# A fused four-layer kernel: FP4 weights decoded in three operations, part of it moved into stage 1, and a softplus polynomial split between VectorE and ScalarE

## The chip, the core and the metric

One NeuronCore of one Trainium2 chip runs the whole kernel in one launch. The metric is device time in microseconds (us). Engines: PE is TensorE (matrix products), DVE VectorE, ACT ScalarE, POOL GpSimd, SP SyncE, which issues most of the DMAs. ScalarE evaluates its functions from loaded tables; the compiler places a table load wherever a function of another set follows.

## The reference, cut to what matters

Four layers, each a cross attention and a feed-forward part with a gated residual. x is (4, 256, 256), that is 1024 tokens of 256 features. The change touches the feed-forward part of layer 0 and the state-space part of layer 3, whose context side is computed early.

```python
# layer 0, feed-forward: W = NVFP4_LUT[4-bit code] * scale of its block of 32
Wg = dequant_nvfp4(gate_W_packed, gate_scales)   # (2048, 256); two codes in each int32
Wu = dequant_nvfp4(up_W_packed, up_scales)
Wd = dequant_nvfp4(down_W_packed, down_scales)   # (256, 2048)
x = x + tanh(g_ffn[0]) * ((gelu(h @ Wg.T) * (h @ Wu.T)) @ Wd.T)      # h = layernorm(x)
# layer 3, attention: a state-space scan over the context
dt = softplus(dt_low @ dt_proj_w.T + dt_proj_b)                      # (4, 256, 256)
state = state * exp(dt * A) + (dt * u) * B_t;  y = (state * C_t).sum() + D * u
```

## The kernel before, in words

The kernel is a row of eight stages, each a block in which every engine has its own instruction list, written by hand; waits on semaphores tie the lists together, and a stage begins when all engines have ended the one before. Each engine keeps to the order of its list.

**Stage 0** is the attention of layer 0. SP loads x, the attention's weights and then, through `load_packed` (L191), the packed codes of gate, up and down (1 MB each) with their scales. The whole FP4 decode stands on VectorE, in six pieces of 128x2048 numbers (`dequant_on_vector`, L199): pieces 0 and 1 are the low and the high code of gate, 2 and 3 of up, 4 and 5 of down. A piece is four instructions: two that shift and mask the low 16 bits of each word into magnitude (L206) and sign (L208), an OR (L210), and one that multiplies the result, read as fp16, by 2^14 and the scale (L218). Piece 0 stands before the softmax's normalisation, piece 1 behind it, pieces 2 to 5 behind the update of x (L323), as the last work of the stage.

**Stage 1** is the feed-forward part of layer 0, with the state-space part of layer 3 laid beside it. The hidden dimension of 2048 is cut into 16 blocks (NHC), the tokens into two halves: 32 units u. For each unit TensorE computes `gate_up(u + 1)` (L511) and then `down(u)` (L524); ScalarE takes gelu of the gate (L445, two units at a time), VectorE multiplies by the up part in `gated(u)` (L645). `down(u)` waits for `gated(u)`, `gate_up(u)` for `gated(u - 2)`. Beside it, for the state-space part: the context's projection (L479), a convolution (L560) and Silu, then the projection of B, C and the step (`project_bc`, L487), whose result VectorE splits into three bf16 parts (`split_rows_1` and `_2`, L574 and L582, in units 0 and 1); ScalarE copies it for a store (L450). `project_steps(k)` (L495) gives the argument of softplus for each half k of the 256 channels: in PSUM at units 2 and 3. Softplus is max(z, 0) + log(1 + exp(-|z|)): ScalarE computes Abs and Exp (`step_exponent`, L422, after units 2 and 4), VectorE the clamp at zero (L595) and log(1 + t) as a polynomial of degree 10, Horner's way (`softplus`, L590), in three parts per k, one part in each of the units 3 to 8. From unit 9 (SCAN0) on, 19 scan groups follow, about one per unit (`scan_group`, L624): TensorE broadcasts a row of B and of C (`row`, L467), ScalarE computes the decays exp(dt * A) (L410), VectorE multiplies, scans (L634), multiplies, and POOL issues a DMA that adds the result to yssm (L690). `add_half` (L616) adds the result of each token half to x.

The loads of stage 1 (L403) are issued by SP when the stage begins. Buffers are cut by hand out of the regions regA, regB and regC.

Of the kernel before, what the change touches and what calls it, by code (L numbers as in the profile page):

```python
# [6 lines left out]

# [5 lines left out]
T = B * S  # L13
NT = T // P
KD = D // P
# [12 lines left out]
I32 = mybir.dt.int32  # L28
F32R = mybir.dt.float32r
# [22 lines left out]
def build(nc, a, out):  # L52
    with ExitStack() as ctx:
# [133 lines left out]
        raw = [regB[:, i * 2048:(i + 1) * 2048].bitcast(I32) for i in range(3)]  # L187
        scl = [regB[:, (3 + i) * 2048:(4 + i) * 2048] for i in range(3)]
# [10 lines left out]
        def dequant_on_vector(dve, v, dq, s_pk, pieces):  # L199

            code, sign = dq
            for n in pieces:
                i, par = divmod(n, 2)
                dve.wait_ge(s_pk[i], 16 * 9)
                lo16 = raw[i].bitcast(U16).rearrange("p (n two) -> p n two", two=2)[:, :, 0]
                v.mark(nc.vector.tensor_scalar(code, lo16, 9 - 4 * par, 0x0E00,  # L206
                                               ALU.logical_shift_left, ALU.bitwise_and))
                v.link(nc.vector.tensor_scalar(sign, lo16, 12 - 4 * par, 0x8000,  # L208
                                               ALU.logical_shift_left, ALU.bitwise_and))
                v.link(nc.vector.tensor_tensor(code, code, sign, ALU.bitwise_or))  # L210
                half = code.bitcast(FP16)
# [11 lines left out]
        def stage0():  # L223
# [6 lines left out]
            dq = [ar.take([4 * HALF], U16), ar.take([4 * HALF], U16)]  # L230
# [4 lines left out]
            s_pk = [sem(f"s0_pk{i}") for i in range(3)]  # L235
            s_aTp, s_aT, s_mix, s_v = sem("s0_aTp"), sem("s0_aT"), sem("s0_mix"), sem("s0_v")
            s_tg = sem("s0_gates")
            with nc.Block("stage0") as block:  # L238
# [59 lines left out]
                def _(dve):  # L298
# [26 lines left out]
                    dequant_on_vector(dve, v, dq, s_pk, range(2, 6))  # L325
# [22 lines left out]
        LDEG = len(L) - 1  # L348

# [3 lines left out]
        def stage1():  # L353
# [13 lines left out]
            zpos = arP.take([KD, T])  # L367
            bcf = arP.take([T])
# [6 lines left out]
            bc32 = arB.take([T])  # L375
# [9 lines left out]
            SP = 3  # L385
            SCAN0 = SP + 3 * KD
# [11 lines left out]
            with nc.Block("stage1") as block:  # L398
# [10 lines left out]
                def _(act):  # L409
# [12 lines left out]
                    def step_exponent(k):  # L422
                        act.wait_ge(s_pre, k + 1)
                        w = (sA, sB)[k]
                        nc.scalar.activation(w, pair, ACT.Abs, bias=cw[:, k, TAPS + 1:TAPS + 2]).then_inc(s_e, 1)
                        act.wait_ge(s_e, k + 1)
                        nc.scalar.activation(dt[:, k, :], w, ACT.Exp, scale=-1.0).then_inc(s_dt, 1)

# [11 lines left out]
                    for u in range(0, NU, 2):  # L440
# [6 lines left out]
                        if u == 0:  # L447
                            nc.scalar.activation(alog, alog, ACT.Exp).then_inc(s_A, 1)
                            act.wait_ge(s_bcs, 1)
# [7 lines left out]
                        if u in (2, 4):  # L457
                            step_exponent(u // 2 - 1)
# [7 lines left out]
                def _(pe):  # L466
# [57 lines left out]
                    def down(u):  # L524
                        c = u % NHC
                        pe.wait_ge(s_itm, u + 1)
                        if u == NHC:
# [10 lines left out]
                    for u in range(NU):  # L538
# [6 lines left out]
                        if u == SP - 1:  # L545
                            project_steps(0)
                        down(u)
# [8 lines left out]
                def _(dve):  # L556
# [33 lines left out]
                    def softplus(k, part):  # L590

                        t, q, w = dt[:, k, :], du[:, k, :], (sA, sB)[k]
                        if part == 0:
# [4 lines left out]
                            v.link(nc.vector.tensor_scalar(q, t, -0.5, None, ALU.add))  # L598
                            v.link(nc.vector.tensor_scalar(w, q, L[LDEG], L[LDEG - 1], ALU.mult, ALU.add))
                            v.link(nc.vector.tensor_tensor(w, w, q, ALU.mult))  # L600
                        for c in {0: (8, ), 1: (7, 6, 5, 4), 2: (3, 2, 1)}[part]:
                            v.link(nc.vector.scalar_tensor_tensor(w, w, L[c], q, ALU.add, ALU.mult))
                        if part == 2:
                            v.link(nc.vector.scalar_tensor_tensor(w, w, L[0], t, ALU.add, ALU.mult))
                            dve.wait_ge(s_max, k + 1)
                            v.link(nc.vector.tensor_tensor(t, w, zpos[:, k, :], ALU.add))
# [46 lines left out]
                    for u in range(NU):  # L653
                        if u == 0:
                            split_rows_1()
                        elif u == 1:
                            split_rows_2()
                        elif u == 2:
# [5 lines left out]
                        elif u < SCAN0:  # L664
# [1541 lines left out]
```

## Time and profile before

| | us |
|---|---|
| median of 3 runs | 976.05 |
| lowest and highest | 972.63, 976.88 |
| the profiled execution | 975.31 |
| its span, first to last instruction | 973.5 |
| VectorE busy | 701.5 (72%) |
| TensorE busy | 638.0 (66%) |
| ScalarE busy | 316.7 (33%) |
| mean granted TensorE clock | 0.798 of full |

Times in the rows are microseconds from the span's start. Stage 0 runs to 64.6, stage 1 from there to about 279. A row of a timeline gives the start, the duration, engine, line, operation, output<-input with their shapes, a count if several were merged, and in brackets how long the engine had been idle before it and what ended that.

### The profile page before, as it was taken

The page shows a single profiled execution, that of the slowest core. Times are in us where ns is not written, and L with a number is a line of the kernel's source. Part 1 is how long each engine was busy: PE and PEld are TensorE (multiplying, and loading weights), DVE is VectorE, ACT ScalarE, POOL GpSimd, SP SyncE. Part 2 cuts the span into 40 slices and gives each one's busy share as a digit, 9 for nine tenths or more (in the row PEclk, how much of TensorE's full clock was granted, in tenths as well). Part 3 has the DMA queues.
Part 4 walks back from the last instruction along what each step waited for, and adds up shares of the span by engine and source line. Part 5 has one row for each costly group of instructions (what it writes and reads, how often), then busy time and mean ns, then how long its engine had stood idle before and what let it go on. Part 6 is the DMA issues. An engine that isn't in the chain of part 4 may idle for free. (4 is left out here: it accounts for less than half of the span.)

```text
span 973.5 us, 9330 instructions
## 1 busy us (share of the span) xinstructions
PE 638.0 (66%) x2790; PEld 400.1 (41%) x2793; DVE 701.5 (72%) x1409; ACT 316.7 (33%) x535; POOL 188.4 (19%) x185
## 2 busy tenths in 40 slices
PE   4419999999954442999183378989880363339980
PEld 2304555555534332568052245555450132235540
DVE  6997698979967755975528849797859887853433
ACT  4004527545222321332223155446630232313210
POOL 0000001111100002442569000000013123004305
PEclk9758999999986665999686578889985576558995
DMA  9300003535566031344300031333445300013314
GB/s 241 91 12 0 6 0 61 91 65 87 87 171 170 0 130 33 109 120 100 112 30 0 0 87 44 87 72 89 110 77 139 78 1 0 0 49 92 93 59 129
DMA packets 57184, 71.17 MB, mean 73 GB/s; under 512 B 14152, under 2 KB 40656, under 8 KB 55984
## 3 DMA queue, kind: packets, MB, share of 16 engines
q1 hardware_dynamic: 44304, 42.52, 15.1%
q0 software_dynamic: 12832, 28.06, 14.6%
q8 instruction: 24, 0.39, 0.2%
q14 instruction: 24, 0.20, 0.1%
HBM read 43.43 MB, written 10.35 MB: 55 GB/s over the span
## 5 line engine op out<-in xcount | busy, mean ns | idle before, releaser
L519 PE MATMUL ps<-hT,regA 128*128 128x512 f32 x256 | 115.3, 593 | 1.0 <-ACT hT L435 1.0
L1762 PE MATMUL ps<-regD,regC 128*34 128x256 f32 x256 | 75.0, 420 | 22.9 <-ACT regD L1627 11.8
L690 POOL DMA_DIRECT2D yssm<-regB x19 | 22.9, 1205 | 245.9 <-DVE regB L642 245.9
L519 PEld LDWEIGHTS ps<-hT,regA 128*128 128x128 f32 x256 | 48.4, 190 | 51.9 <-issue 46.7
L530 PE MATMUL ps<-regA,regC 128*128 128x256 f32 x256 | 64.2, 396 | 6.9 <-DVE regC L649 5.4
L530 PEld LDWEIGHTS ps<-regA,regC 128*128 128x128 f32 x256 | 47.9, 194 | 31.9 <-DVE regC L649 20.7
L1160 POOL DMA_INDIRECT regA<-h_rows,regA x31 | 29.4, 947 | 141.9 <-DVE regA L1380 111.0
L445 ACT ACTIVATE regC<-ps 128x512 f32<-128x512 f32 x32 | 19.1, 597 | 92.8 <-PE ps L519 88.1
L1627 ACT ACTIVATE regD<-ps 128x512 f32<-128x512 f32 x64 | 38.1, 596 | 32.1 <-PE ps L1748 31.4
L634 DVE TENSOR_TENSOR_SCAN regB<-regB 128x512 f32<-128x512 f32 x38 | 44.5, 1212 | 2.8
L1762 PEld LDWEIGHTS ps<-regD,regC 128*34 128x34 f32 x256 | 25.1, 118 | 48.3 <-issue 19.1
L1869 DVE TENSOR_REDUCE regC<-ps 128x4 f32<-128x960 f32 x64 | 39.8, 684 | 5.0 <-PE ps L1717 5.0
L1706 PE MATMUL ps<-ident,regA 128*128 128x128 f32 x192 | 32.4, 340 | 16.3 <-DVE regA L1860 11.9
L1575 POOL DMA_DIRECT2D yssm<-regC x13 | 15.8, 1214 | 138.7 <-DVE regC L1910 116.9
L1706 PEld LDWEIGHTS ps<-ident,regA 128*128 128x128 f32 x192 | 29.0, 179 | 19.6 <-issue 13.1
L1160 POOL DMA_INDIRECT regB<-h_rows,regB x23 | 21.9, 954 | 77.7 <-DVE regB L1380 46.3
L1386 DVE TENSOR_TENSOR regB<-regB,ps 128x176 f32<-128x176 f32 x23 | 7.8, 338 | 40.3 <-ACT regB L1197 40.3
L175 PE MATMUL ps<-ident,h 128*128 128x128 f32 x112 | 20.5, 361 | 23.7 <-DVE h L158 22.9
L163 ACT ACT_TABLE_LOAD x7 | 9.0, 1283 | 80.8 <-PEq L238 43.4
L1254 PE MATMUL ps<-regB,regA 128*128 x124 | 35.0, 407 | 0.0
L1254 PE MATMUL ps<-regA,regB 128*128 x92 | 32.7, 480 | 0.0
L649 DVE TENSOR_TENSOR regC<-regC,ps 128x512 f32<-128x512 f32 x32 | 21.9, 683 | 14.1 <-ACT regC L445 13.5
(387 smaller groups left out, 1565.9 us busy)
## 6 DMA issues: line engine op xcount, KB each, us to landing
yssm<-regB POOLq DMA_DIRECT2D x19, 512.0 KB, 5.0
regC<-bc_rows SPq DMA_DIRECT2D x26, 256.0 KB, 3.9
yssm<-regC POOLq DMA_DIRECT2D x13, 512.0 KB, 6.9
regB<-in_L_w SPq DMA_DIRECT2D x4, 1088.0 KB, 11.7
y_rows<-regA SPq DMA_DIRECT2D x31, 128.0 KB, 2.5
y_rows<-regB SPq DMA_DIRECT2D x23, 128.0 KB, 1.7
regB<-in_L_w SPq DMA_DIRECT2D x1, 2176.0 KB, 12.9
regC<-in_L_W SPq DMA_DIRECT2D x2, 1024.0 KB, 5.8
```

What stands on the lines that cost most here:

```text
L175: last = nc.tensor.transpose(o, src[:, t, k * P:(k + 1) * P], (idn or ident)[:, :])
L519: m = nc.tensor.matmul(ps[:, 2 + 2 * (u % 2) + j, :], w[:, k * 2048 + c * P:k * 2048 + (c + 1) * P], hT[:, k, hf * HALF:(hf + 1) * HALF], ...
L530: m = nc.tensor.matmul(ps[:, t // 2, (t % 2) * D:(t % 2 + 1) * D], itm[:, u % 2, t * P:(t + 1) * P], WDv[:, c // 2, c % 2, :], start=(c == ...
L634: v.mark(nc.vector.tensor_tensor_scan(hs[:, k, :], dA[:, g % RD, k].rearrange("p b l -> p (b l)"), dBu[:, k, :], 0.0, ALU.mult, ALU.add))
L649: nc.vector.tensor_tensor(itm[:, u % 2, :], gel[:, u % 2, :], ps[:, 3 + 2 * (u % 2), :], ALU.mult).then_inc(s_itm, 1)
L690: nc.gpsimd.dma_start(y, hc[:, g % 2], accum_op=ALU.add).then_inc(s_y, 16)
L1160: nc.gpsimd.indirect_dma_start(xg[:, b % NG, :], None, h_rows, bass.IndirectOffsetOnAxis(rowid[:, b:b + 1], 0)).then_inc(s_got[b % NG], 16)
L1254: m = nc.tensor.matmul(ps[:, block_banks(u)[1], 0:GU], lhs, W[:, bass.ds(at + k * GU, GU)], start=k == 0, stop=k == KD - 1)
L1627: nc.scalar.activation(prob[:, n % 4, :], ps[:, 4 + n % 2, :], ACT.Exp, scale=SCALE4).then_inc(s_p, 1)
L1706: m = nc.tensor.transpose(ps[:, blk // 2, c0:c0 + P], flat(src[:, b % 2, t])[:, blk * P:(blk + 1) * P], ident[:, :])
L1762: m = nc.tensor.matmul(ps[0:VW, 6 + j % 2, (n % 2) * S:(n % 2 + 1) * S], vaug[:, 2 * b + kt, hd, :], prob[:, n % 4, kt * S:(kt + 1) * S], ...
L1869: nc.vector.tensor_reduce(dst[:, :, :, j], sc[:, :, :, lo:hi], AX.X, ALU.max, negate=True).then_inc(s_mx, 1)
```

## The change

The decode becomes three instructions per piece: one that shifts the 32-bit word left by 28 - 4*par and arithmetically right by 19, one mask with 0x8E00, both on 32-bit integers in one buffer `code`, and the scaling, which reads every second 16-bit number of it. Stage 0 keeps pieces 0 to 3; pieces 4 and 5 (down) move to units 0 and 1 of stage 1, and `down(0)` and `down(1)` wait for them (s_down_w). Raw codes and scales of down are therefore placed where stage 1 doesn't write before unit 5. `split_rows_1` and `_2` move to units 2 and 3, with the sign of A and the products with D, and the copy for the store behind gelu(3). `project_steps(0)` moves behind `down(3)`, `project_steps(1)` behind `down(5)`; `step_exponent` stands after the units 4 and 6. The polynomial is written as a product of five quadratics (t + a)^2 + b: ScalarE computes each square from t with the bias a (ten in all, two buffers `sqr`, given back by s_sqd), VectorE one step (square + b) * w for each, and then one multiply-add in place of the last two operations. Softplus takes the units 5 to 8, two parts per k. SCAN0 stays 9, and everything from there is as before. POOL sets five constants when stage 1 begins.

```diff
@@ -184,8 +187,9 @@
 
         NHC = 2048 // P
         WG, WU, WD = (regA[:, i * 4096:(i + 1) * 4096] for i in range(3))
-        raw = [regB[:, i * 2048:(i + 1) * 2048].bitcast(I32) for i in range(3)]
-        scl = [regB[:, (3 + i) * 2048:(4 + i) * 2048] for i in range(3)]
+        raw = [regB[:, i * 2048:(i + 1) * 2048].bitcast(I32) for i in (0, 1, 3)]
+        scl = [regB[:, i * 2048:(i + 1) * 2048] for i in (2, 5, 4)]
+        s_pk = [sem(f"packed_{nm}") for nm in ("gate", "up", "down")]
         WDv = WD.rearrange("p (c a n) -> p c a n", c=NHC // 2, a=2)
 
         def load_packed(sp, s_pk):
@@ -198,17 +202,14 @@
 
         def dequant_on_vector(dve, v, dq, s_pk, pieces):
 
-            code, sign = dq
+            code = dq
             for n in pieces:
                 i, par = divmod(n, 2)
                 dve.wait_ge(s_pk[i], 16 * 9)
-                lo16 = raw[i].bitcast(U16).rearrange("p (n two) -> p n two", two=2)[:, :, 0]
-                v.mark(nc.vector.tensor_scalar(code, lo16, 9 - 4 * par, 0x0E00,
-                                               ALU.logical_shift_left, ALU.bitwise_and))
-                v.link(nc.vector.tensor_scalar(sign, lo16, 12 - 4 * par, 0x8000,
-                                               ALU.logical_shift_left, ALU.bitwise_and))
-                v.link(nc.vector.tensor_tensor(code, code, sign, ALU.bitwise_or))
-                half = code.bitcast(FP16)
+                v.link(nc.vector.tensor_scalar(code, raw[i], 28 - 4 * par, 19,
+                                               ALU.logical_shift_left, ALU.arith_shift_right))
+                v.link(nc.vector.tensor_scalar(code, code, 0x8E00, None, ALU.bitwise_and))
+                half = code.bitcast(FP16).rearrange("p (n two) -> p n two", two=2)[:, :, 0]
                 if i < 2:
                     o, q, sc = (WG, WU)[i][:, par * 2048:(par + 1) * 2048], half, scl[i]
                 else:
@@ -227,12 +228,11 @@
             w = ar.take([2, C])
             bqk = ar.take([2])
             nmx, den = ar.take([NT]), ar.take([NT])
-            dq = [ar.take([4 * HALF], U16), ar.take([4 * HALF], U16)]
+            dq = ar.take([4 * HALF], I32)
             s_c, s_x, s_in = sem("s0_context"), sem("s0_x"), sem("s0_constants")
             s_var, s_sd, s_h = sem("s0_var"), sem("s0_sd"), sem("s0_h")
             s_proj, s_qk, s_en, s_mx = sem("s0_proj"), sem("s0_qk"), sem("s0_en"), sem("s0_mx")
             s_exp, s_att, s_hTp, s_hT = sem("s0_exp"), sem("s0_att"), sem("s0_hTp"), sem("s0_hT")
-            s_pk = [sem(f"s0_pk{i}") for i in range(3)]
             s_aTp, s_aT, s_mix, s_v = sem("s0_aTp"), sem("s0_aT"), sem("s0_mix"), sem("s0_v")
             s_tg = sem("s0_gates")
             with nc.Block("stage0") as block:
@@ -322,7 +322,7 @@
                         xb = x[:, 2 * b:2 * b + 2, :]
                         nc.vector.scalar_tensor_tensor(xb, ps[:, b, :].rearrange("p (t m) -> p t m", t=2),
                                                        tg[:, 0:1], xb, ALU.mult, ALU.add)
-                    dequant_on_vector(dve, v, dq, s_pk, range(2, 6))
+                    dequant_on_vector(dve, v, dq, s_pk, range(2, 4))
 
 
 
@@ -346,6 +346,10 @@
         L = (0.810930216216, -0.288527111915, 0.132609761683, -0.0676876229793, 0.0366112232653, -0.0205713852149,
              0.0118477560374, -0.0067441046525, 0.00401169096238, -0.00325434358357, 0.00198669635839)
         LDEG = len(L) - 1
+        upper = [z for z in np.roots(L[::-1]) if z.imag > 0]
+        assert len(upper) == LDEG // 2
+        QUADS = [(float(-upper[i].real - 0.5), float(upper[i].imag ** 2)) for i in (3, 2, 0, 1, 4)]
+        NQ = len(QUADS)
 
 
 
@@ -364,15 +368,18 @@
             LP = S + TAPS - 1
             xpad = arP.take([KD, B, LP])
             sA, sB = arP.take([T]), arP.take([T])
-            zpos = arP.take([KD, T])
-            bcf = arP.take([T])
+            arQ = Arena(regB[:, 3 * 2048:5 * 2048])
+            zpos, sqr = arQ.take([KD, T]), arQ.take([2, T])
             in_w = arB.take([KD * P])
             xp_w = arB.take([KD, 3 * NBC + DTR])
             dt_w = arB.take([D])
             dtl = arB.take([T])
             bc1, bc2 = arB.take([T], BF16), arB.take([T], BF16)
             self_ = arB.take([NBC])
-            bc32 = arB.take([T])
+            bc32, bcf = arB.take([T]), arB.take([T])
+            code = arB.take([4 * HALF], I32)
+            sqc = arB.take([NQ])
+            s_down_w, s_sqc, s_sq, s_sqd = (sem("s1_" + n) for n in ("down_weights", "sq_bias", "sq", "sq_used"))
             s_bc32, s_bcd, s_late, s_softp = sem("s1_bc32"), sem("s1_bc_stored"), sem("s1_late"), sem("s1_softplus")
             s_var, s_sd, s_h, s_hTp, s_hT = (sem("s1_" + n) for n in ("var", "sd", "h", "hTp", "hT"))
             s_gu, s_gel, s_itm, s_down, s_add, s_v = (sem("s1_" + n) for n in ("gu", "gel", "itm", "down", "add", "v"))
@@ -382,8 +389,8 @@
                 sem("m_" + n) for n in "w xi xc u z xp bcs pre e dt max A skip".split())
             NU = 2 * NHC
             NGR = 2 * NST - NLATE
-            SP = 3
-            SCAN0 = SP + 3 * KD
+            SP = 5
+            SCAN0 = SP + 2 * KD
             LAST = NU - 2
             unit_of = [SCAN0 + g * (LAST - SCAN0) // NGR for g in range(NGR)]
 
@@ -425,6 +432,12 @@
                         nc.scalar.activation(w, pair, ACT.Abs, bias=cw[:, k, TAPS + 1:TAPS + 2]).then_inc(s_e, 1)
                         act.wait_ge(s_e, k + 1)
                         nc.scalar.activation(dt[:, k, :], w, ACT.Exp, scale=-1.0).then_inc(s_dt, 1)
+                        act.wait_ge(s_dt, k + 1)
+                        for i in range(NQ):
+                            n = k * NQ + i
+                            if n >= 2:
+                                act.wait_ge(s_sqd, n - 1)
+                            nc.scalar.activation(sqr[:, n % 2, :], dt[:, k, :], ACT.Square, bias=sqc[:, i:i + 1]).then_inc(s_sq, 1)
 
                     norm_on_scalar(act, s_var, s_sd)
                     for k in range(KD):
@@ -446,6 +459,7 @@
                                                  ACT.Gelu_apprx_tanh).then_inc(s_gel, 1)
                         if u == 0:
                             nc.scalar.activation(alog, alog, ACT.Exp).then_inc(s_A, 1)
+                        if u == 2:
                             act.wait_ge(s_bcs, 1)
                             nc.scalar.copy(bc32[0:NBC, :], pair[0:NBC, :]).then_inc(s_bc32, 1)
                         if u == SCAN0 + 1:
@@ -454,8 +468,10 @@
                                 nc.scalar.copy(dst[:, :, :], src[:, :, HALF:T]).then_inc(s_late, 1)
                             act.wait_ge(s_ready, 1)
                             nc.scalar.copy(alog_late[:, :, :], alog).then_inc(s_late, 1)
-                        if u in (2, 4):
-                            step_exponent(u // 2 - 1)
+                        if u in (SP - 1, SP + 1):
+                            if u == SP - 1:
+                                act.wait_ge(s_sqc, NQ)
+                            step_exponent((u - SP + 1) // 2)
                         if u >= SCAN0 - 2:
                             due = [g for g in range(NGR) if unit_of[g] <= u + 3]
                             for g in due[issued:]:
@@ -524,6 +540,8 @@
                     def down(u):
                         c = u % NHC
                         pe.wait_ge(s_itm, u + 1)
+                        if u < 2:
+                            pe.wait_ge(s_down_w, u + 1)
                         if u == NHC:
                             pe.wait_ge(s_add, 1)
                         for t in range(TPH):
@@ -542,9 +560,9 @@
                             row(g, 1)
                         for g in groups_at(u)[:1]:
                             row(g, 0)
-                        if u == SP - 1:
+                        down(u)
+                        if u == SP - 2:
                             project_steps(0)
-                        down(u)
                         for g in groups_at(u)[:1]:
                             row(g, 1)
                         for g in groups_at(u)[1:]:
@@ -595,15 +613,15 @@
                             nc.vector.tensor_scalar(zpos[:, k, :], pair, cw[:, k, TAPS + 1:TAPS + 2], 0.0,
                                                     ALU.add, ALU.max).then_inc(s_max, 1)
                             dve.wait_ge(s_dt, k + 1)
-                            v.link(nc.vector.tensor_scalar(q, t, -0.5, None, ALU.add))
-                            v.link(nc.vector.tensor_scalar(w, q, L[LDEG], L[LDEG - 1], ALU.mult, ALU.add))
-                            v.link(nc.vector.tensor_tensor(w, w, q, ALU.mult))
-                        for c in {0: (8, ), 1: (7, 6, 5, 4), 2: (3, 2, 1)}[part]:
-                            v.link(nc.vector.scalar_tensor_tensor(w, w, L[c], q, ALU.add, ALU.mult))
-                        if part == 2:
-                            v.link(nc.vector.scalar_tensor_tensor(w, w, L[0], t, ALU.add, ALU.mult))
+                        for i in ((0, 1, 2), (3, 4))[part]:
+                            n = k * NQ + i
+                            dve.wait_ge(s_sq, n + 1)
+                            v.link(nc.vector.scalar_tensor_tensor(w, sqr[:, n % 2, :], QUADS[i][1], t if i == 0 else w,
+                                                                  ALU.add, ALU.mult))
+                            dve.sem_inc(s_sqd, 1)
+                        if part == 1:
                             dve.wait_ge(s_max, k + 1)
-                            v.link(nc.vector.tensor_tensor(t, w, zpos[:, k, :], ALU.add))
+                            v.link(nc.vector.scalar_tensor_tensor(t, w, L[LDEG], zpos[:, k, :], ALU.mult, ALU.add))
                             v.link(nc.vector.tensor_tensor(q, t, u_ssm[:, k, :], ALU.mult))
                             dve.sem_inc(s_softp, 1)
 
@@ -651,18 +669,20 @@
 
                     gated(0)
                     for u in range(NU):
-                        if u == 0:
+                        if u < 2:
+                            dequant_on_vector(dve, v, code, s_pk, (4 + u,))
+                            dve.sem_inc(s_down_w, 1)
+                        elif u == 2:
                             split_rows_1()
-                        elif u == 1:
+                        elif u == 3:
                             split_rows_2()
-                        elif u == 2:
                             dve.wait_ge(s_A, 1)
                             v.link(nc.vector.tensor_scalar(alog, alog, -1.0, None, ALU.mult))
                             for k in range(KD):
                                 nc.vector.tensor_scalar(yssm[:, k, :], u_ssm[:, k, :], cw[:, k, TAPS + 2:TAPS + 3], None,
                                                         ALU.mult).then_inc(s_skip, 1)
-                        elif u < SCAN0:
-                            softplus(*divmod(u - SP, 3))
+                        elif SP <= u < SCAN0:
+                            softplus(*divmod(u - SP, 2))
                             if u == SCAN0 - 1:
                                 v.link(nc.vector.memset(dA[:, :, :, :, 0:1].rearrange("p a b c d -> p (a b c) d"), 0.0))
                                 dve.sem_inc(s_ready, 1)
@@ -679,6 +699,8 @@
 
                 @block.gpsimd
                 def _(pool):
+                    for i in range(NQ):
+                        nc.gpsimd.memset(sqc[:, i:i + 1], QUADS[i][0]).then_inc(s_sqc, 1)
                     for g in range(NGR):
                         hf, n = divmod(g, NST)
                         pool.wait_ge(s_hc, g + 1)
```

## Rows read from the trace of the kernel before

**Rows 1.** The page's first part: busy us, share of the span, instructions.
```profile
PE 638.0 (66%) x2790; PEld 400.1 (41%) x2793; DVE 701.5 (72%) x1409; ACT 316.7 (33%) x535; POOL 188.4 (19%) x185
```
**Rows 2.** Windows: length, busy us of each engine, granted clock, DMA share, GB/s.
```profile
18.50:40.70 22.20, 11.78 (x58) 9.08 (x56) 21.57 (x38) 3.18 (x10) 0.00 (x0) 0.87 0.69 165
40.70:64.60 23.90, 0.00 (x0) 0.00 (x0) 23.52 (x17) 0.00 (x0) 0.00 (x0) 0.50 0.00 0
...
87.70:106.30 18.60, 18.60 (x55) 9.78 (x53) 11.27 (x15) 6.67 (x8) 0.00 (x0) 1.00 0.03 7
106.30:147.00 40.70, 38.06 (x113) 20.65 (x111) 37.83 (x37) 13.42 (x16) 0.00 (x0) 1.00 0.00 1
```
**Rows 3.** Timeline of VectorE, end of stage 0 and start of stage 1.
```profile
40.72 1.22 DVE L206 TENSOR_SCALAR regC<-regB 128x2048 uint16<-128x2048 uint16 x1
41.85 1.22 DVE L208 TENSOR_SCALAR regC<-regB 128x2048 uint16<-128x2048 uint16 x1
43.10 1.23 DVE L210 TENSOR_TENSOR regC<-regC 128x2048 uint16<-128x2048 uint16 x1
44.36 2.29 DVE L218 SCALAR_TENSOR_TENSOR regA<-regC,regB 128x2048 f32<-128x2048 f16 x1
...
65.13 2.71 DVE L145 BATCH_NORM_STATS2 lnst<-x 128x6 f32<-128x256 f32 x8 [0.54 <-PEq L238]
```
**Rows 4.** Waits of 64 to 150 us: who waited for whom, total, times, longest.
```profile
PE ps L483 <- DMA regB<-in_m_sel: 34.0, 1, 34.0
```
**Rows 5.** Groups of VectorE's instructions by form: busy us, mean ns | idle before.
```profile
L602 DVE SCALAR_TENSOR_TENSOR regB<-regB,regC 128x1024 f32<-128x1024 f32 x16 | 19.6, 1223 | 0.4
...
L867 DVE TENSOR_SCALAR regA<-regA 128x2048 f32<-128x2048 f32 x2 | 2.5, 1228 | 0.1
```
**Rows 6.** Timeline of VectorE in stage 1.
```profile
87.73 0.69 DVE L649 TENSOR_TENSOR regC<-regC,ps 128x512 f32<-128x512 f32 x1 [3.03 <-ACT regC L445]
...
126.86 0.69 DVE L649 TENSOR_TENSOR regC<-regC,ps 128x512 f32<-128x512 f32 x1 [0.21 <-DVE regC L607]
127.47 1.28 DVE L595 TENSOR_SCALAR regB<-ps,regC 128x1024 f32<-128x1024 f32 x1
...
147.47 1.28 DVE L629 TENSOR_TENSOR regB<-regC,ps 128x512 f32<-128x512 f32 x2
...
155.18 1.29 DVE L629 TENSOR_TENSOR regB<-regC,ps 128x512 f32<-128x512 f32 x2 [1.77 <-PE ps L475]
```
**Rows 7.** Timeline of TensorE: down (L530) of units 0, 1 and 9, a step projection (L502).
```profile
92.79 1.89 PE L530 MATMUL ps<-regA,regC 128*128 128x256 f32 x8
...
97.95 1.89 PE L530 MATMUL ps<-regA,regC 128*128 128x256 f32 x8
...
103.21 1.98 PE L502 MATMUL ps<-regB 8*128 8x512 f32 x4
...
147.61 3.66 PE L530 MATMUL ps<-regA,regC 128*128 128x256 f32 x8 [2.97 <-DVE regC L649]
```
**Rows 8.** Timeline of ScalarE: Abs, Exp and gelu of stage 1; Square of stage 4.
```profile
105.22 1.11 ACT L425 ACTIVATE regB<-ps,regC 128x1024 f32<-128x1024 f32 x1 [1.31 <-PE ps L502]
106.36 1.28 ACT L427 ACT_TABLE_LOAD   x1
107.65 1.06 ACT L427 ACTIVATE regC<-regB 128x1024 f32<-128x1024 f32 x1
...
110.58 0.60 ACT L445 ACTIVATE regC<-ps 128x512 f32<-128x512 f32 x1 [0.57 <-PE ps L519]
...
507.81 0.63 ACT L1593 ACTIVATE regC<-regA 128x512 f32<-128x512 f32 x1 [4.09 <-DVE regD L1821]
```
**Rows 9.** Windows of TensorE: length, busy us, granted clock, DMA share, GB/s.
```profile
144.60:147.60 3.00, 0.04 (x1) 1.00 0.00 0
147.60:149.50 1.90, 1.89 (x5) 0.50 0.00 0
...
190.50:191.90 1.40, 0.07 (x2) 1.00 0.01 1
```

More of the change, by code:

```diff
@@ L6 @@
 from contextlib import ExitStack
+import numpy as np
 import concourse.bass as bass
@@ L28 @@
 I32 = mybir.dt.int32
+I16 = mybir.dt.int16
 F32R = mybir.dt.float32r
```

## The prediction

> **What bounds the kernel now.** I read the page first: no engine fills the span [rows 1], so a change is worth what it is worth in its own stage. The windows of the two stages that the diff touches come next [rows 2]. From 18.5 to 64.6 us VectorE has work nearly all the time. From 40.7 to 64.6 it is alone: TensorE does nothing, no transfer moves (so every load of stage 0 has landed), and ScalarE is idle. In stage 1 the picture turns over: from 87.7 to 106.3 TensorE is busy for the whole stretch and VectorE for 11.3 of 18.6 us; from 106.3 to 147.0 both are nearly full. So the end of stage 0 hangs on VectorE alone, and the first ten hidden blocks of stage 1 on TensorE, with VectorE a few us behind. The decode rows [rows 3] show what fills the lonely stretch: four groups of four instructions, then stage 1 starts 0.5 us behind the last. TensorE waited 34 us for stage 1 to begin [rows 4]; that wait ends by a load that is issued when the stage starts, so it moves with the stage.
>
> **Part 1, the decode itself.** One piece takes now, from the first instruction at 40.72 to the end of the fourth at 46.65 and 0.04 us to the next, 5.97 us: 1.13, 1.25, 1.26 and 2.33 [rows 3]. New: two one-source instructions on 2048 four-byte integers and the same scaling. The trace has no integer instruction of that size and width. Its nearest rows are the 16-bit shift-and-mask at 1.22 us [rows 3], the 4-byte float one at 1.228 [rows 5] (same count, one source, SBUF to SBUF), and, as the other bound, the 2.29 us of an operation that takes one element a cycle [rows 3]. I take 1.23: width, count and sources are those of the float row. With 0.03 to 0.04 us per link, a piece is 1.27 + 1.27 + 2.33 = 4.87 us, 1.10 less. The scaling reads every second 16-bit number; it is at 2.29 already and the strided 16-bit reads of the first two run twice as fast, so nothing is added. The Trainium skill (VectorE: DVE Perf Modes, "What auto-detection actually checks") asks for one source and destination in SBUF and says nothing of integers, which speaks for 1.23; its table lists only bf16 and fp32.
>
> **Part 2, stage 0.** Four pieces stay (0 and 1 earlier, 2 and 3 in the lonely stretch): 4 x 1.10 = 4.4 us. The pieces before 40.7 count too, since VectorE is busy 21.6 of 22.2 us there [rows 2], and the work between them is ready when it comes. Pieces 4 and 5 leave: 2 x 5.97 = 11.9 us. Stage 0 ends 16.3 us earlier. The waits are on loads that landed before 40.7; placing buffers elsewhere costs nothing.
>
> **Part 3, units 0 to 4 of stage 1** (times as in the trace of before, without the 16.3). Piece 4 starts after gated(0), 88.4 [rows 6], ends at 93.3, and the signal costs 0.2 (the 0.21 us idle behind L607, which also has a signal in front [rows 6]). So down(0) starts at 93.4 and not 92.79 [rows 7]. Piece 5 runs from 94.2 to 99.1, down(1) starts at 99.3 and not 97.95: 1.4 us late. Then TensorE runs free: a unit is 97.95 - 92.79 = 5.16 us, the step projection 1.9 [rows 7]. Three units and one projection bring gate_up(5) to its end at 116.7, gelu(5) [rows 8] to 117.5. split_rows and the skip products, moved to units 2 and 3, fit beside: they need some 9 us on VectorE between 99.4 and 111, where it was idle for 7 us before [rows 2]. The copy to bc32 is ready at 110, the projection that needs it starts at 111.4.
>
> **Part 4, the polynomial.** Before, a k took 147.47 - 127.47 = 20.0 us from its clamp to the next stage of work [rows 6], all on VectorE, three gated products among them. Now each k has five steps of 1.22 + 0.04 + 0.17 for the signal = 1.43 us, and two more operations of 1.26 [rows 5]. That is 7 operations against 14: some 14 us of VectorE work less for both k, against 9.9 us of decode more. But the order matters more than the sum. The five squares stand on ScalarE **ahead of the next two gelus**, there are only two buffers, so the fifth square waits for the third step. Abs 1.11, table load 1.28, Exp 1.06 [rows 8], Square: the only one in the trace is 0.63 for 512 columns, Abs with the same kind of bias 1.11 for 1024 [rows 8]; I take 1.11. From 117.5 this gives the first step at 122.1. Three steps: 126.4. Then VectorE has nothing: square 1.11, table load 1.28, gelu 0.6, gated(6) at 129.4 (before: 126.86 [rows 6]). Two steps, two operations, signals: gated(7) 135.5. Clamp 1.2, three steps, the same gap of 3.0: gated(8) 144.6. Another 6.4: gated(9) at 151.0.
>
> TensorE must wait for gated(8) with down(8), 3.9 us. Before it waited 2.97 us for gated(9), and down(9) then took 3.66 instead of 1.89 us [rows 7], at the lower clock level, 1.2 GHz [rows 9]; a wait of 1.3 us left the clock at full [rows 9]. So I charge 1.8 us to down(8): it starts at 145.3, gate_up(10) ends at 152.2, and the first scan starts at 152.6, not 147.47: 5.1 us late. Of this 1.8 comes back, since the second scan group waited 1.77 us [rows 6] for the slow down(9), which now has its slow stretch in front. From there the order is unchanged, TensorE and VectorE are in step, and the delay is carried to the stage's end: **3.4 us**.
>
> ScalarE's exp of the decays waits for VectorE as before. The five memsets on POOL are over long before ScalarE looks for them. Nothing is added to SP's queue; the store of bc_rows goes out 11 us later in the stage and nobody in the stage waits for it. The POOL queue's accumulations shift with the scans.
>
> **Sum.** -16.3 + 3.4 = -12.9 us. The profiled execution took 975.3 us (its span 973.5), so 962.4; the median of the runs is 0.7 higher, 976.05, so about **963.0**.
>
> Bounds of the stage 1 term: below, nothing at all lost and even the 2.97 us wait [rows 7] gone (-3, 956); above, both decode pieces (9.9) on the path once more instead of 1.4, +8.5 more (971). The signals, 10 x 0.17, and the clock, 1.8, are the parts I know least; without both it is near 0.
>
> **Rivals.**
> **A, stage 1 loses nothing** (the signals and the clock dip cost nothing, TensorE's backlog hides the gaps): 975.3 - 16.3 + 0.7 = 959.7. For: TensorE was the fuller engine there. Against: gelu(6) stands behind five squares by the code. 0.12.
> **B, the integer operations take 2.29 each.** A piece is 7.0 us. Stage 0 gains 11.9 - 4 x 1.03 = 7.8; stage 1 loses 3.4 + 2 x 2.1 = 7.6. Time 975.8, no change. Against it are both one-source rows at 1.22. 0.08.
> **C, slower: TensorE's clock stays at its lower level** from the first gap at down(6) until the scans. Four units at half speed cost 4 x 5.16 = 20.6, less the 1.8 counted: 18.8 more, 982. It decides if the gaps of 1.2, 1.0 and 3.9 us keep the clock from coming back between them. Against it: after 2.97 us idle it was low for less than 4 us, and 1.3 us did not lower it [rows 9]. 0.03.
> **D, Square is not in the table set of Exp:** one more load of 1.28 per k on the chain, +2.6, 965.6. Against it: Square at 507.81 and Abs at 105.22 ran with no load in front [rows 8]. 0.08.
> **E, a table switch costs twice its row.** Four switches lie on the new chain, 4 x 1.28 = 5.1, 968.1. The row shows Exp starting 0.01 us behind the load [rows 8]. 0.03. The Trainium skill (ScalarE: Activation LUTs, "What ACT_TABLE_LOAD costs") gives 1.28 for the load and some 1.38 for a drain; by it, an estimate, the four would cost 5.5 more. The trace disagrees with the drain.
>
> **Numbers.** The forecast has 0.66. The range 958.5 to 967.5 holds it, A and D; B, C and most of E are outside. About 0.5% is what a measurement of this kernel can tell from no change, 4.9 us. Faster: forecast, A, D, E, 0.89. Same: B, 0.08. Slower: C, 0.03.
>
> **What would show it.** The windows: stage 0 ends near 48.3. The decode's integer operations at 1.23, no 2.29 among them but the scaling. Idle of about 3 us before gated(6) and gated(8), put down to L445 on ScalarE; Square at about 1.1 and no load before it; 0.2 us between the steps. TensorE waiting some 4 us before down(8) and a clock of 0.5 behind it. First scan near 136, last add of stage 1 near 266. I am wrong in kind if gated(6) follows the third step directly, if TensorE waits long at down(0) or down(1), or if stages from 2 on change their length.

## The result

The changed kernel takes 963.12 us (median of 4 runs, 962.32 to 965.07) against 976.46 before; the ratio estimated from the runs is 0.9858 (95% interval 0.9825 to 0.9891); the plain quotient of the two medians, 0.9863, lies inside it. The forecast was 963.0. Its profiled execution has a span of 962.1 us against 973.5.

**The profile after.** The windows of the changed kernel, cut as in [rows 2] (the five pairs of numbers are TensorE, its weight loads, VectorE, ScalarE and GpSimd):

```profile
39.60:49.30 9.70, 0.00 (x0) 0.00 (x0) 9.49 (x7) 0.00 (x0) 0.00 (x0) 0.56 0.00 0
49.30:71.70 22.40, 12.95 (x37) 5.93 (x38) 15.86 (x36) 10.75 (x13) 0.23 (x5) 0.81 0.06 13
71.70:90.30 18.60, 17.72 (x54) 9.70 (x53) 16.68 (x15) 4.59 (x6) 0.00 (x0) 1.00 0.00 0
90.30:136.60 46.30, 41.42 (x115) 22.04 (x114) 27.48 (x31) 28.15 (x30) 0.00 (x0) 0.96 0.01 3
```

The lonely stretch of VectorE shrank from 23.9 to 9.7 us. In the last window VectorE is no longer nearly full (27.5 of 46.3 us, where it was 37.8 of 40.7), ScalarE's work doubled, and still the window is 5.6 us longer. The timeline of VectorE shows a piece of the decode, the start of stage 1, and the units of the polynomial:

```profile
39.61 1.22 DVE L209 TENSOR_SCALAR regC<-regB 128x2048 int32<-128x2048 int32 x1
40.86 1.23 DVE L211 TENSOR_SCALAR regC<-regC 128x2048 int32<-128x2048 int32 x1
42.12 2.29 DVE L219 SCALAR_TENSOR_TENSOR regA<-regC,regB 128x2048 f32<-128x2048 f16 x1
44.45 1.23 DVE L209 TENSOR_SCALAR regC<-regB 128x2048 int32<-128x2048 int32 x1
...
49.80 2.71 DVE L148 BATCH_NORM_STATS2 lnst<-x 128x6 f32<-128x256 f32 x8 [0.54 <-PEq L238]
...
71.72 0.69 DVE L667 TENSOR_TENSOR regC<-regC,ps 128x512 f32<-128x512 f32 x1 [3.03 <-ACT regC L458]
...
107.71 2.60 DVE L619 SCALAR_TENSOR_TENSOR regB<-regB 128x1024 f32<-128x1024 f32 x2
113.49 0.69 DVE L667 TENSOR_TENSOR regC<-regC,ps 128x512 f32<-128x512 f32 x1 [3.18 <-ACT regC L458]
...
128.47 0.69 DVE L667 TENSOR_TENSOR regC<-regC,ps 128x512 f32<-128x512 f32 x1 [3.18 <-ACT regC L458]
...
136.58 1.28 DVE L647 TENSOR_TENSOR regB<-regC,ps 128x512 f32<-128x512 f32 x2 [1.09 <-PE ps L491]
```

A piece takes 44.45 - 39.61 = 4.84 us where it took 5.97 [rows 3]. Before gated(6) (113.49) and gated(8) (128.47) VectorE idles 3.18 us for a gelu. ScalarE's timeline shows what stands in front of that gelu: the five squares (L440), of which the third to the fifth wait for VectorE's steps, and a table load. TensorE's shows down(0), down(1) and what the second gap does to down(8); its windows there (the granted clock is the third number from the end) show that the lower level, 0.50 of full or 1.2 GHz, began within 1 us behind the wait:

```profile
104.00 1.06 ACT L434 ACTIVATE regC<-regB 128x1024 f32<-128x1024 f32 x1
105.09 2.19 ACT L440 ACTIVATE regB<-regC,regB 128x1024 f32<-128x1024 f32 x2
107.66 1.15 ACT L440 ACTIVATE regB<-regC,regB 128x1024 f32<-128x1024 f32 x1 [0.38 <-DVEq L621]
109.03 1.15 ACT L440 ACTIVATE regB<-regC,regB 128x1024 f32<-128x1024 f32 x1 [0.23 <-DVEq L621]
110.40 1.15 ACT L440 ACTIVATE regB<-regC,regB 128x1024 f32<-128x1024 f32 x1 [0.22 <-DVEq L621]
111.57 1.28 ACT L458 ACT_TABLE_LOAD   x1
112.86 1.25 ACT L458 ACTIVATE regC<-ps 128x512 f32<-128x512 f32 x2
```
```profile
77.34 1.97 PE L548 MATMUL ps<-regA,regC 128*128 128x256 f32 x8 [0.39 <-DVEq L674]
...
83.23 1.97 PE L548 MATMUL ps<-regA,regC 128*128 128x256 f32 x8 [0.49 <-DVEq L674]
...
129.21 3.55 PE L548 MATMUL ps<-regA,regC 128*128 128x256 f32 x8 [3.51 <-DVE regC L667]
```
```profile
125.60:129.20 3.60, 0.11 (x1) 0.00 (x0) 0.73 (x2) 3.55 (x5) 0.00 (x0) 1.00 0.00 0
129.20:131.10 1.90, 1.89 (x5) 1.56 (x6) 1.75 (x2) 1.03 (x1) 0.00 (x0) 0.57 0.00 0
131.10:132.50 1.40, 1.40 (x4) 1.11 (x4) 1.25 (x2) 0.00 (x0) 0.00 (x0) 0.50 0.00 0
```

**Where the time went**, between marks that both traces have (stages 2 to 7 begin at 279.07 and 266.52):

| stretch | before | after | change |
|---|---|---|---|
| start to piece 0 | 18.53 | 19.69 | +1.16 |
| piece 0 to stage 1 | 46.60 | 30.11 | -16.49 |
| stage 1 to gated(0) | 22.60 | 21.92 | -0.68 |
| gated(0) to the first scan | 59.74 | 64.86 | +5.12 |
| first scan to stage 2 | 131.60 | 129.94 | -1.66 |
| stages 2 to 7 | 694.43 | 695.58 | +1.15 |

The sum is -11.4 us for this pair of executions; the medians differ by 13.3. The last row holds no changed instruction: stage 3, the same code in all runs, takes 129.7 to 133.2 us in the traces of this study (130.5 before, 132.7 in the changed kernel). The first row holds none either, but the change moved the buffers that are being loaded there, and the row is not settled. Most of the 1.16 us are in TensorE's first eight matmuls, at a full granted clock and with the DMA engines busy throughout, before and after:

```profile
8.06 5.18 PE L274 MATMUL ps<-ctxT,regC 128*128 128x512 f32 x8 [8.06 <-DMA ctxT<-in_ctxT]
```
```profile
8.33 6.21 PE L274 MATMUL ps<-ctxT,regC 128*128 128x512 f32 x8 [8.33 <-DMA ctxT<-in_ctxT]
```

In the other eleven traces they take 5.5 to 6.7 us, and piece 0 starts at 19.1 to 20.6. The one trace of the kernel before lies below all of them, so a small price of the moved buffers is neither shown nor excluded.

### The profile page after: what moved, and what is told of

It is laid out like the page before. It is cut to its first block and busy times, and to the rows that moved or that the text cites. A ratio compares the mean times of both kernels' runs of the same rounds, so it can differ in the third digit from the quotient of the medians.

```text
span 962.1 us, 9340 instructions
## 1 busy us (share of the span) xinstructions
PE 641.3 (67%) x2790; PEld 403.6 (42%) x2793; DVE 679.5 (71%) x1389; ACT 327.9 (34%) x545; POOL 189.1 (20%) x190
## 5 line engine op out<-in xcount | busy, mean ns | idle before, releaser
L1784 PEld LDWEIGHTS ps<-regD,regC 128*34 128x34 f32 x256 | 25.2, 119 | 47.6 <-issue 16.3
L1728 PE MATMUL ps<-ident,regA 128*128 128x128 f32 x192 | 32.2, 339 | 16.3 <-DVE regA L1882 11.9
```

Of the source, the lines that this page charges most:

```text
L1728: m = nc.tensor.transpose(ps[:, blk // 2, c0:c0 + P], flat(src[:, b % 2, t])[:, blk * P:(blk + 1) * P], ident[:, :])
L1784: m = nc.tensor.matmul(ps[0:VW, 6 + j % 2, (n % 2) * S:(n % 2 + 1) * S], vaug[:, 2 * b + kt, hd, :], prob[:, n % 4, kt * S:(kt + 1) * S], ...
```

## The experiments

Theory 1: all that stage 1 loses comes from two late downs (the decode) and from gelus that stand behind squares which themselves wait for VectorE. Rivals: TensorE sets the pace and covers the gaps; or the decode alone makes the stage late. All edits are made on the changed kernel. The short table gives, for each, the distance from the start of gated(0) to that of gated(8), of gated(9), of the first scan group and of stage 2, in us, and the duration of TensorE's down(8), all from one profiled execution. Times are medians where several runs were made (changed, second square, all three), else one run; the runs were made on several chips, on which the kernel before had medians of 975.65 to 976.98.

| run | gated(8) | gated(9) | first scan | stage 2 | down(8) | time |
|---|---|---|---|---|---|---|
| before | 50.53 | 59.14 | 59.74 | 191.34 | 1.99 | 976.46 |
| changed | 56.75 | 63.08 | 64.86 | 194.80 | 3.55 | 963.12 |
| gelu behind second square | 52.41 | 58.73 | 59.34 | 189.27 | 1.99 | 956.25 |
| five buffers | 53.04 | 59.37 | 59.97 | 189.90 | 1.99 | 959.16 |
| four-operation decode | 58.69 | 65.38 | 68.02 | 198.05 | 3.78 | 970.01 |
| down pieces in stage 0 | 55.40 | 61.73 | 62.34 | 192.27 | 1.99 | 970.83 |
| Horner | 60.25 | 70.12 | 70.73 | 203.58 | 1.99 | 973.85 |
| direct signal | 56.08 | 62.18 | 64.20 | 194.50 | 3.10 | 964.26 |
| TensorE kept busy | 58.45 | 64.78 | 65.38 | 195.30 | 1.99 | 966.38 |
| all three | 51.03 | 57.51 | 58.11 | 188.40 | 1.89 | 957.84 |

**The gelus behind the second square.**

```diff
+                            if i == 1:
+                                gelu(SP + 1 + 2 * k)
```


> gelu(6) and gelu(8) stand behind the second square instead of behind the fifth; nothing else changes. Theory 1 (the two gaps come from the gelus that stand behind squares which wait for VectorE): the idle of 3.18 us before gated(6) and before gated(8) falls to under 1 us, TensorE's wait before down(8) from 3.51 to about 1 us, down(8) takes 1.9 instead of 3.55 us, gated(0) to the first scan product 59 to 60 us instead of 64.9, gated(0) to the start of stage 2 some 5.5 us less than 194.8, the time about 957.5. Rival, TensorE's own work sets the pace of these units and the gaps are covered: under 1 us is gained, 962 to 963. Rival, the decode in units 0 and 1 is what made the stage late: the same, under 1 us.

Measured: 956.25 us, ratio to before 0.9787 (0.9748 to 0.9826). TensorE's wait before down(8) fell to 0.95 us. VectorE's timeline of this run at gated(6) and gated(8), and TensorE's at down(8):

```profile
111.16 0.69 DVE L673 TENSOR_TENSOR regC<-regC,ps 128x512 f32<-128x512 f32 x1 [0.22 <-DVE regB L625]
...
123.58 0.69 DVE L673 TENSOR_TENSOR regC<-regC,ps 128x512 f32<-128x512 f32 x1 [0.22 <-DVE regB L625]
```
```profile
124.32 1.99 PE L554 MATMUL ps<-regA,regC 128*128 128x256 f32 x8 [0.95 <-DVE regC L673]
```

Both gaps are gone (waits of 1.32 and 0.55 us before the third steps took their place) and stage 1 ends 5.53 us earlier, more than the 3.46 that the change had lost there. Both rivals fall: TensorE did not cover the gaps, and the decode, untouched here, was not the main thing that made the stage late (its own share, 1.35 us, is measured below).

**Five buffers.**

```diff
+            sq_bufs = [sqr[:, 0, :], sqr[:, 1, :], arP.take([T])] + [regB[:, j * T:(j + 1) * T] for j in range(2)]
-                            if n >= 2:
-                                act.wait_ge(s_sqd, n - 1)
+                            if n >= 5:
+                                act.wait_ge(s_sqd, n - 4)
```


> Five buffers for the squares instead of two, the gelus stay behind the fifth square. Theory 1: squares no longer wait for steps, so the gap before gated(6) becomes about 2 us (it waits for five squares, a table load and a gelu in one row), that before gated(8) goes away, since the squares of the second half run ahead during the first half's steps; gated(0) to the first scan about 60 us. If the gap were due to the row of squares alone and not to the waits between ScalarE and VectorE, both gaps would stay near 3 us and nothing would be gained.

Measured: the first scan at 59.97, and smaller gaps before gated(6) and gated(8):

```profile
112.47 0.69 DVE L668 TENSOR_TENSOR regC<-regC,ps 128x512 f32<-128x512 f32 x1 [2.03 <-ACT regC L459]
...
124.89 0.69 DVE L668 TENSOR_TENSOR regC<-regC,ps 128x512 f32<-128x512 f32 x1 [0.63 <-ACT regC L459]
```

So about two thirds of the first gap (2.03 of 3.18 us) stay with the row of five squares, and most of the second (2.55 of 3.18) was the waiting for buffers. This is one run.

**The decode of before, in the new places.**

```diff
+                v.mark(nc.vector.tensor_scalar(mag, lo16, 9 - 4 * par, 0x0E00,
+                                               ALU.logical_shift_left, ALU.bitwise_and))
+                v.link(nc.vector.tensor_scalar(sign, lo16, 12 - 4 * par, 0x8000,
+                                               ALU.logical_shift_left, ALU.bitwise_and))
+                v.link(nc.vector.tensor_tensor(mag, mag, sign, ALU.bitwise_or))
```


> The decode of before (two 16-bit shift-and-masks, an OR, the scaling) in the places of the changed kernel. Theory 1: a piece takes 5.97 instead of 4.84 us; stage 0 is 4 x 1.1 = 4.4 us longer from piece 0 to its end; in stage 1 down(0) and down(1) start 1.1 and 1.9 us later than in the changed kernel, counted from gated(0), and the whole 1.9 us reaches the first scan (66.8 us behind gated(0)). Sum +6.3 us, about 969.5. Rival, units 0 and 1 have slack for it: +4.4 us only, 967.5.

Measured: piece 0 to stage 1 34.63 us, +4.52; down(1) +1.93, and gated(8) still +1.94. The rival falls: units 0 and 1 had no slack for the longer pieces. From there it lost 1.2 us more than expected, to the first scan +3.16: TensorE's windows of this run show the low clock over 6 us, beginning inside the wait.

```profile
132.80:136.30 3.50, 0.02 (x1) 0.87 0.00 0
136.30:140.00 3.70, 3.70 (x9) 0.50 0.00 0
140.00:142.00 2.00, 2.00 (x4) 0.50 0.00 0
```

**The down pieces back in stage 0.**

```diff
-                    dequant_on_vector(dve, v, dq, s_pk, range(2, 4))
+                    dequant_on_vector(dve, v, dq, s_pk, range(2, 6))
```


> Pieces 4 and 5 go back to the end of stage 0 in their new form; split_rows stays in units 2 and 3, the polynomial stays new. Theory 1: stage 0 is 2 x 4.84 = 9.7 us longer, down(0) and down(1) come 0.6 and 1.4 us earlier behind gated(0), the first scan 1.4 us earlier (63.5 us behind gated(0)); sum +8.3 us, about 971.5. Rival, the move costs more inside stage 1 than the two late downs show (the later split and projections): the first scan comes over 3 us earlier and the sum is under +6.7 us.

Measured: stage 0 +9.69; gated(8) and gated(9) 1.35 us earlier, as the late downs say. The first scan came 2.52 us earlier, under the 3 us that the rival asked for, and the 1.17 us above 1.35 are the clock: the same wait of 3.51 us before down(8) was followed by **no** low clock, 1.99 us. TensorE's windows of the wait and of down(8):

```profile
134.40:137.80 3.40, 0.00 (x0) 1.00 0.00 0
137.80:139.80 2.00, 1.93 (x9) 1.00 0.00 0
```

**The polynomial of before.**

```diff
+                        for c in {0: (8, 7, 6, 5), 1: (4, 3, 2, 1)}[part]:
+                            v.link(nc.vector.scalar_tensor_tensor(w, w, L[c], q, ALU.add, ALU.mult))
...
-                            nc.scalar.activation(sqr[:, n % 2, :], dt[:, k, :], ACT.Square, bias=sqc[:, i:i + 1]).then_inc(s_sq, 1)
```


> The changed kernel with the polynomial of before: Horner's way on VectorE alone, 14 operations per half of the channels in two parts, no squares on ScalarE; the new decode and the move stay. Theory 1: VectorE alone then sets the pace of units 5 to 8, without the 3 us gaps but with 16.6 instead of 9.5 us of work per half; gated(9) comes 6 to 7 us later and the first scan 70 to 71 us behind gated(0) instead of 64.9; time about 969. Rival, the gaps give back what the squares take off VectorE: the first scan within 1.5 us of 64.9.

Measured: first scan at 70.73, inside the expectation, so the rival falls; but stage 2 at 203.58 and the time 973.85, 5 us above it. Three of them are in the scans, 132.85 us instead of 129.94: TensorE waited 4.23 us for gated(9), behind the first `row`, and down(9) and gate_up(11) ran slowly. (Before down(7) it had waited 4.16 us already, with a slow down(7), 3.78 us, behind.)

```profile
143.24 3.78 PE L542 MATMUL ps<-regA,regC 128*128 128x256 f32 x8 [4.23 <-DVE regC L661]
146.81 0.63 PE L485 MATMUL ps<-regC 96*128 96x512 bf16 x1
147.24 4.57 PE L529 MATMUL ps<-hT,regA 128*128 128x512 f32 x8
```

**The direct signal.**

```diff
-                            dve.sem_inc(s_sqd, 1)
+                                                           ALU.add, ALU.mult).then_inc(s_sqd, 1)
+                            dve.wait_ge(s_sqd, n + 1)
```


> Each of the ten steps signals s_sqd itself and VectorE waits on that, instead of a link and then a separate signal instruction. Theory 1: 0.1 us less between steps and for each square that waits for a step, so the first scan comes 1.0 us earlier (63.9 us behind gated(0), if the clock dip behind the gap is the same). Rival, the signal costs nothing: no change of the distance from gated(0) to gated(9), 63.1 us.

Measured: gated(9) 0.90 us earlier, the first scan 0.66; stage 2 0.30. The rival falls, but little of it arrives. The low clock fell here as well:

```profile
128.88 3.10 PE L548 MATMUL ps<-regA,regC 128*128 128x256 f32 x8 [3.29 <-DVE regC L667]
```

It cost TensorE the same 1.7 us in down(8) and the gate_up behind it as in the changed kernel. With it the first scan waits for TensorE, whose row starts from gated(8), 0.67 us earlier, and not for gated(9), 0.90 earlier. The other 0.36 is lost in the scans, 130.30 us instead of 129.94: VectorE idles 0.52 us behind the first scan operation. This comes again in both executions of "all three", the other kernel with direct signals, and in no other; why was not tried.

**TensorE kept busy in the wait.**

```diff
+                        if u == SCAN0 - 1:
+                            pe.wait_ge(s_max, KD)
+                            for r in range(4):
+                                nc.tensor.matmul(ps[:, 6, :], WG[:, 0:P], hT[:, 0, 0:HALF], start=True, stop=True)
```


> TensorE does four matmuls of 128x512 into a free bank in front of down(8), in the 3.5 us that it waits for gated(8); their result is overwritten unread. If the idle is what let the clock fall: no low clock, down(8) 1.9 to 2.0 instead of 3.55 us, the first scan 1.2 us earlier, 63.7 us behind gated(0), since VectorE is ready no sooner. If down(8) was slow for another reason (its operands, VectorE's accesses): it stays at 3.5 us.

Measured: down(8) takes 1.99 us, as expected if the idle is what lets the clock fall. But the run with the down pieces in stage 0 had 1.99 us behind the full wait too, so this one run does not prove that the four matmuls kept the clock up. The first scan is at 65.38 and not 63.7, but gated(1) was already 1.69 us late: the projection before it met a low clock of its own (5.38 instead of 3.68 us), which lies before the edit. 65.38 - 1.69 = 63.69. TensorE's rows of this run, and its clock in the slow projection:

```profile
69.37 5.38 PE L507 MATMUL ps<-regC,regB 128*104 128x512 f32 x8 [1.92 <-ACT regC L451]
...
126.78 3.60 PE L545 MATMUL ps<-hT,regA 128*128 128x512 f32 x8
130.46 1.99 PE L552 MATMUL ps<-regA,regC 128*128 128x256 f32 x8
```
```profile
70.00:74.00 4.00, 4.00 (x7) 0.59 0.00 0
```

**All three together** (five buffers, gelus behind the third square, direct signals).

> Five buffers, the gelus behind the third square, direct signals. Theory 1: no idle of over 0.3 us before gated(6) and gated(8), the first scan 58.1 us behind gated(0) (59.3 with the gelus behind the second square, 59.7 in the kernel before), stage 2 at 188.0 behind gated(0); time about 955. If TensorE's own work (its row from down(1) on, 45 us with two step projections) is already the bound, no more than 0.3 us under the run with the gelus behind the second square.

Measured: first scan at 58.11, stage 2 at 188.40; the idle before gated(6) and gated(8) is 0.23 us; 957.84 us over 6 runs that reach from 953.6 to 963.06, ratio 0.9809 (0.9762 to 0.9855). The first scan is 1.23 us before that of the version with the second square, so TensorE's own work was not the bound there yet; 0.87 us of it reaches stage 2. The time, 2.8 us above the expected 955, did not show it. So three kernels ran once more on one chip:

> The changed kernel once more, beside the two best versions on one chip. Gated(0) to gated(9) 63.1 us as before; from there 64.9 or 63.7 us to the first scan, by whether the low clock falls on the gap before down(8). Time about 963.

> The version with the gelus behind the second square once more. First scan 59.3 us behind gated(0), 5.5 us before the changed kernel's; time about 957.

> Five buffers, gelus behind the third square, direct signals, once more. First scan 58.1 us behind gated(0), 1.2 us before the version with the gelus behind the second square; time about 956. If its median of 957.8 against that version's 956.3 were a real loss outside stage 1, it shows again with both on one chip.

Measured, ratios to before: changed 962.62 us, 0.985 (0.9815 to 0.9886); gelus behind the second square 956.64, 0.9798 (0.9762 to 0.9835), which leaves out one execution of 971.19; all three 956.57, 0.9788 (0.9756 to 0.982). The distances from gated(0) came again within 0.02 us, down(8) of the changed kernel at 3.65. From gated(0) to stage 2 "all three" has 0.86 us less than the gelus behind the second square, too little for its time to show; the loss suspected in it did not come again. Both versions beat the kernel before and the changed kernel.

## Why the prediction was right

**The decode** was right: 1.22 and 1.23 us for the integer operations, 4.84 per piece (4.87 forecast), and the stage 16.49 us shorter (16.3). Rival B, 2.29 us, falls. That the buffers could be placed elsewhere at no cost, the other part of the stage's term, is not settled, as said under the table of stretches.

**Units 0 to 4** were right: gated(0) to down(0) 5.62 us and to down(1) 11.51, against 5.06 and 10.22 [rows 7]: 0.6 and 1.3 late. The run with the pieces in stage 0 gives 1.35 us as their whole price.

**The polynomial** was right, and by its mechanism: gaps of 3.18 us (3.0), which moving the two gelus removes. Two sizes were off and cancelled: Square with its bias takes 1.145 us (ten of them, 11.3 us; 1.11 forecast), and a step with its signal 1.37 instead of 1.43. Two steps stand at 107.71 with 2.60 us for both. Rivals A and D fall; no load stands before a square, as in the rows of ScalarE above. The Horner run prices the split in its new places, units 5 to 8: 8.8 us of stage 1, of which 2.9 are the slow down(9) and its wait in the scans.

**The clock** was the step that is right only by luck. I charged 1.8 us to down(8) and took 1.8 back in the scans; measured were 1.6 on down(8), of which 1.17 reached the first scan, since VectorE was ready no sooner, and 1.66 less in the scans. The reason given for the 1.8 in the scans fails: it was said to come back because the slow stretch had moved in front of down(8). In the four runs without a low clock before the scans (second square, five buffers, down pieces in stage 0, TensorE kept busy) they take 129.9 us as well, and they take 132.85 in the Horner run, where TensorE again waits over 4 us for gated(9). So the 1.66 us are a gain of the shorter way from gated(8) to gated(9), 6.33 us instead of 8.61, which leaves down(9) without its 2.97 us wait; they come whether the clock falls at down(8) or not. VectorE's rows of gated(8) and gated(9), before and after:

```profile
138.26 0.69 DVE L649 TENSOR_TENSOR regC<-regC,ps 128x512 f32<-128x512 f32 x1
...
146.87 0.69 DVE L649 TENSOR_TENSOR regC<-regC,ps 128x512 f32<-128x512 f32 x1 [0.22 <-DVE regB L667]
```
```profile
128.47 0.69 DVE L667 TENSOR_TENSOR regC<-regC,ps 128x512 f32<-128x512 f32 x1 [3.18 <-ACT regC L458]
...
134.80 0.69 DVE L667 TENSOR_TENSOR regC<-regC,ps 128x512 f32<-128x512 f32 x1 [0.22 <-DVE regB L687]
```

Nor is the charge at down(8) a fixed one: the wait alone does not decide, since behind the same 3.51 us the clock fell in the changed kernel both times and with the four-operation decode, and did not with the down pieces in stage 0. What the runs support is a cost of 0, of 1.2, or (decode run, 3.16 - 1.93 us more than the changed kernel) of 2.4 us at the first scan. What decides between them stays open. Rival C falls: the low level lasted some 6 us at most behind the gap. Rival E falls: gelu starts 0.01 us behind its load (111.57, 1.28 long, and 112.86).

**The sum**, +3.4 us for stage 1 from gated(0), was measured as +3.46. The match of the whole, 963.0 and 963.12, is closer than the mechanism can claim: in the profiled pair the four middle stretches gained 13.7 us and not 12.9, of which 0.68 are the stretch from stage 1 to gated(0), at which the forecast put nothing and which varies by 1.3 us over the runs; the first and the last row took back 2.3. Between the medians it is 13.3.

## What to carry to other kernels

When work is moved onto an engine with free time, look at what stands behind it in that engine's list: here 11 us of squares were cheap, and their place in front of two gelus whose inputs were ready cost 5.5 us (the low clock behind the gap included), more than the whole 3.5 us that the stage had lost. Put the instruction that another engine waits for at the first point where the list would wait anyway. And take each engine's waits, not its busy share, as the measure: VectorE's busy time fell by 10 us in a window that grew by 5.6.

## What was not expected of the hardware

TensorE's clock came up at very different times at the start of stage 1, after an idle of nearly the same length (17.5 and 18.3 us): the windows of its first work show 3.4 us at the low level (1.2 GHz) in the changed kernel, and 8.8 us in the run with five buffers, whose instructions are the same up to there.

```profile
54.40:57.80 3.40, 3.38 (x4) 0.50 0.00 0
57.80:60.00 2.20, 1.10 (x3) 1.00 0.00 0
```
```profile
54.00:62.80 8.80, 7.41 (x9) 0.50 0.00 0
62.80:64.00 1.20, 1.20 (x10) 0.78 0.00 0
```

One and the same kernel did both: with the gelus behind the second square, TensorE's second group of matmuls there takes 1.99 us in one execution and 3.78 in the other. Stage 1 to gated(0) is 21.92 and 22.64 us in the two runs above, 21.8 to 23.0 over all traces. Stage 3 varies more, 129.7 to 133.2 us, and by 1.4 and 1.8 us between two executions of one kernel (second square, all three). Both will be part of what spreads the times of one kernel by several us, but only profiled executions have stages, so their share is not shown; why stage 3 varies was not tried.
